# Softmax of a cross-attention in a four-part block: exponential taken on the transposed tile, sums by products with ones, division behind the values

## The reference

```python
def _L1_xattn_ref(q, k, v, mask, Wq, bq, Wk, bk, Wv, bv, Wo, bo):   # 16 heads of 16, 64 keys
    qh, kh, vh = (proj(q, Wq, bq), proj(k, Wk, bk), proj(v, Wv, bv))
    scores = jnp.einsum('bhqd,bhkd->bhqk', qh, kh) / jnp.sqrt(jnp.float32(D_K))
    scores = jnp.where(mask == 0, jnp.float32(-1000000000.0), scores)
    attn = jax.nn.softmax(scores, axis=-1)
    x = jnp.einsum('bhqk,bhkd->bhqd', attn, vh)
    x = x.transpose(0, 2, 1, 3).reshape(N, -1, NUM_HEADS * D_K)
    return x @ Wo.T + bo
x = x + _L1_xattn_ref(_layernorm(x, axis=-1), ctx_1024, ctx_1024, mask_1x1xSxS2_ik1, ...)
x = x + _L1_ffn_ref(_layernorm(x, axis=-1), ...)
```

## Time and profile before

| what | value |
|---|---|
| time, median of 3 runs | 870.63 us (866.11 to 880.41) |
| the profiled execution's own time | 869.87 us |
| its span, first to last instruction | 868.1 us |
| TensorE busy (share of the span) | 783.3 us (90%) |
| VectorE busy | 453.0 us (52%) |
| ScalarE busy | 254.9 us (29%) |
| GpSimd busy | 181.8 us (21%) |
| second attention and gate, about 563 to 676 us | 113 us |
| in it: PE, DVE, ACT, POOL busy | 90.64, 91.55, 58.39, 54.30 us |

### The profile page before, as it was taken

How to read it: one execution, slowest core, us unless ns; L and a number is a source line. 1 busy time by engine, 2 the same in 40 slices (tenths; PEclk the granted TensorE clock), 3 DMA queues, 4 the chain that set the end, 5 groups by cost and what they waited for, 6 DMA issues and landing times.

```text
span 868.1 us, 11371 instructions
## 1 busy us (share of the span) xinstructions
PE 783.3 (90%) x4207; PEld 636.9 (73%) x4207; DVE 453.0 (52%) x866; ACT 254.9 (29%) x500; POOL 181.8 (21%) x180
## 2 busy tenths in 40 slices
PE   5999797888898999999999999978787399999996
PEld 4665475667687878887888788845566399999995
DVE  3565759796772394349335833497966511111111
ACT  1534213022311222123112312256534043333331
POOL 3022224240200020002000200176531212222221
PEclk9989988989899999999999999999979599999999
DMA  9951600000400000000000000053013477666640
GB/s 313 384 185 69 271 1 2 0 1 17 178 2 1 2 2 3 2 2 2 2 2 2 2 2 3 2 237 151 27 46 113 160 261 219 209 211 216 213 160 0
DMA packets 20525, 79.69 MB, mean 92 GB/s; under 512 B 3053, under 2 KB 12400, under 8 KB 15664
## 3 DMA queue, kind: packets, MB, share of 16 engines
q1 hardware_dynamic: 17504, 70.44, 23.5%
q0 software_dynamic: 2944, 8.13, 2.4%
HBM read 72.27 MB, written 18.74 MB: 105 GB/s over the span
## 4 chain that ended last, share of the span: by engine, by line
PE 70%; DVE 21%; issue 4%; ACT 3%; DMA 1%; POOL 0%; DVEq 0%; SPq 0%; ACTq 0%; POOLq 0%
PE ps L1063 29%; PE ps L1769 10%; PE ps L1781 9%; PE ps L526 4%; PE ps L498 3%; DVE head_max L1611 2%; DVE any_bits L307 2%; DVE stats L282 2%; DVE f_ha_hi L1183 1%; DVE f_raw L1177 1%; DVE c_tok L1612 1%; PE ps L555 1%; PE ps L480 1%; PE ps L1221 1%; DVE a_tok L847 1%
## 5 line engine op out<-in xcount | busy, mean ns | idle before, releaser
L1151 ACT ACTIVATE f_raw<-ps,cols 128x512 f32<-128x512 f32 x96 | 66.2, 690 | 261.7 <-PE ps L1063 242.6
L1063 PE MATMUL ps<-f_hb_hi,fh 128*128 128x512 f32 x256 | 101.2, 395 | 2.5 <-DVE inexact L327 2.5
L1063 PE MATMUL ps<-f_ha_hi,fh 128*128 128x512 f32 x256 | 99.9, 390 | 2.3 <-ACT f_raw L1151 2.3
L1063 PE MATMUL ps<-f_hb_lo,fh 128*128 128x512 f32 x256 | 100.6, 393 | 0.0
L1063 PE MATMUL ps<-f_ha_lo,fh 128*128 128x512 f32 x256 | 99.6, 389 | 0.0
L1769 PEld LDWEIGHTS ps<-xsT,ew 128*128 128x128 f32 x736 | 87.0, 194 | 2.8 <-DVE xsT L1896 1.7
L1769 PE MATMUL ps<-xsT,ew 128*128 128x128 f32 x736 | 87.5, 278 | 1.0 <-DVE xsT L1896 1.0
L1829 ACT ACTIVATE hT<-ps,ew 128x128 f32<-128x128 f32 x184 | 52.5, 369 | 106.2 <-PE ps L1769 96.6
L1781 PE MATMUL ps<-ew,hT 128*128 x368 | 83.3, 380 | 0.0
L1183 DVE CAST f_ha_hi<-f_raw 128x512 fp32r<-128x512 f32 x64 | 31.9, 498 | 89.4 <-ACT f_raw L1151 88.3
L1781 PEld LDWEIGHTS ps<-ew,hT 128*128 128x128 f32 x368 | 68.2, 190 | 8.7 <-issue 0.2
(11 more groups left out here) (235 smaller groups left out, 1280.7 us busy)
## 6 DMA issues: line engine op xcount, KB each, us to landing
ew<-in_ew SPq DMA_DIRECT2D x23, 1028.0 KB, 5.7
fh<-fh_copy SPq DMA_DIRECT2D x2, 4096.0 KB, 14.8
ew<-in_ew SPq DMA_DIRECT2D x1, 8192.0 KB, 23.6
fw<-fw_copy SPq DMA_DIRECT2D x3, 1024.0 KB, 6.8
eb<-in_eb SPq DMA_DIRECT2D x23, 128.0 KB
x_res<-in_x SPq DMA_DIRECT2D x4, 512.0 KB, 10.6
rows<-x_res SPq DMA_DIRECT2D x4, 512.0 KB, 3.3
rows<-xn_e SPq DMA_DIRECT2D x4, 512.0 KB, 3.1
```

The costliest lines, as they stand in the source:

```text
L1063: ins = nc.tensor.matmul(out, *((xk, wk) if swap else (wk, xk)), start=(k == 0 and part == 0), stop=(k == w.shape[1] - 1 and part == 1))
L1151: nc.scalar.activation(f_raw[:, m % 3, :], ps[:, ring_bank(n), :], ACT.Silu if m < KH else ACT.Gelu, scale=col(("w1_s", "h1_s", "h2_s")[m ...
```

## The change

The softmax of the second attention is taken in another order.

- `c_tok` has one buffer; `subtract_max` is as before. `probabilities(b, j)` now transposes one tile's undivided logits, eight groups of 128 by 128, four into bank 0 and four into bank 1, and ACT takes the exponential while it copies them to `c_pT` (`exponentials`). ACT's in-place exponential, its plain copies and DVE's copies of the last batch are gone.
- `invert_sum` and `divide` are gone. `heads` runs, beside each of the value products, a second product of the same size with ones (`vmask`) as the weights; each head's sum comes out in banks 6 and 7, repeated over the head's 16 rows. `invert_sums` on DVE takes the reciprocals of those banks, 128 by 512 each, two a batch, to `c_sums`, and `scale_heads` on POOL multiplies `c_oT` by them.
- The last batch does this in two halves of 256 tokens (`last_heads`): DVE takes reciprocal and product straight from PSUM, POOL takes no part.
- All the orders are rewritten. Transposes of batch `b` now follow its own scores, heads and projection of batch `b - 1` lie in the iteration of batch `b`; a projection lags by one batch, not by two.

The core of the diff:

```diff
-        c_tok = [at(f"c_tok{i}", [P, TT, H1, KEYS], kb) for i, kb in enumerate((157.5, 101.5))]
+        c_tok = at("c_tok", [P, TT, H1, KEYS], 157.5)
+        c_sums = at("c_sums", [P, NG1, S], 113.5)
...
-            def divide(b, j):
-                pool.wait_ge(c_inv, TT * b + j + 1)
-                p = c_tok[b % 2][:, j]
-                pool.tensor_tensor(p, p, head_sum[:, j, :].unsqueeze(2).broadcast_to([P, H1, KEYS]), ALU.mult)\
-                    .then_inc(c_prob, 1)
+            def scale_heads(b):
+                for o in range(NG1):
+                    pool.wait_ge(c_pv_out, NG1 * b + o + 1)
+                    pool.wait_ge(c_inv, NG1 * b + o + 1)
+                    pool.tensor_tensor(c_oT[:, o, :], c_oT[:, o, :], c_sums[:, o, :], ALU.mult).then_inc(c_heads, 1)
...
+            def probabilities(b, j):
+                n = b * TT + j
+                pe.wait_ge(c_sub, n + 1)
+                if j == 0:
+                    if b < LAST:
+                        pe.wait_ge(c_q_out, NG1 * (b + 2))
+                    else:
+                        pe.wait_ge(c_pv_out, NG1 * b)
+                for h in range(2):
+                    if j:
+                        pe.wait_ge(c_pT_out, 2 * (n - 1) + h + 1)
+                    for m in range(TT):
+                        heads = c_tok[:, j, 8 * h + 2 * m:8 * h + 2 * m + 2, :].rearrange("p a k -> p (a k)")
+                        ins = nc.tensor.transpose(ps[:, h, m * P:(m + 1) * P], heads, ident)
                     ins.then_inc(c_pT_full, 1)
+
+            def heads_and_sums(b, o, columns, heads_out, sums_out):
+                for q in range(TT):
+                    m = q // 2 * TT + 2 * o + q % 2
+                    rows_ = slice(q * 2 * DH1, (q + 1) * 2 * DH1)
+                    nc.tensor.matmul(heads_out[rows_], v1_blocks[:, b % 2, o * TT + q, :], c_pT[:, m, columns],
+                                     start=True, stop=True)
+                for q in range(TT):
+                    m = q // 2 * TT + 2 * o + q % 2
+                    rows_ = slice(q * 2 * DH1, (q + 1) * 2 * DH1)
+                    ins = nc.tensor.matmul(sums_out[rows_], con("vmask", 2 * DH1), c_pT[:, m, columns],
+                                           start=True, stop=True)
+                return ins
...
+            def last_heads(hf):
+                if hf == 0:
+                    pe.wait_ge(c_values, NG1 * B)
+                    pe.wait_ge(c_sub, TT * LAST + 3)
+                pe.wait_ge(c_pT_out, 2 * TT * LAST + 4 * (hf + 1))
+                for o in range(NG1):
+                    bank = (2 if hf == 0 else 0) + o
+                    ins = heads_and_sums(LAST, o, slice(hf * D, (hf + 1) * D), ps[:, bank, 0:D], ps[:, bank, D:2 * D])
+                ins.then_inc(c_pv_full, 1)
...
+            for b in range(LAST):
                 scores(b, 0)
+                if b:
+                    heads(b - 1)
                 scores(b, 1)
-                if b < LAST:
-                    attn1_columns(pe, b + 1)
-                if b >= 2:
-                    project(b - 2, 0)
-                    project(b - 2, 1)
-                if b < LAST:
-                    attn1_queries(pe, b + 1)
+                attn1_columns(pe, b + 1)
+                attn1_queries(pe, b + 1)
                 scores(b, 2)
...
+                    project(b - 1, 0)
+                    project(b - 1, 1)
                 scores(b, 3)
...
+                probabilities(b, 0)
+                probabilities(b, 1)
+                if b:
+                    project(b - 1, 2)
+                probabilities(b, 2)
+                if b:
+                    project(b - 1, 3)
+                probabilities(b, 3)
+            scores(LAST, 0)
+            heads(LAST - 1)
+            scores(LAST, 1)
+            scores(LAST, 2)
+            probabilities(LAST, 0)
+            project(LAST - 1, 0)
+            probabilities(LAST, 1)
+            project(LAST - 1, 1)
+            scores(LAST, 3)
+            last_heads(0)
+            project(LAST - 1, 2)
+            probabilities(LAST, 2)
+            project(LAST - 1, 3)
+            probabilities(LAST, 3)
+            project(LAST, 0)
+            project(LAST, 1)
             gate_columns(0)
...
+            last_heads(1)
...
+            def exponentials(b, j):
+                for h in range(2):
+                    act.wait_ge(c_pT_full, 2 * (b * TT + j) + h + 1)
+                    if j == 0 and b:
+                        act.wait_ge(c_pv_full, NG1 * b)
+                    nc.scalar.activation(c_pT[:, h * TT:(h + 1) * TT, j * P:(j + 1) * P],
+                                         ps[:, h, :].rearrange("p (m n) -> p m n", m=TT), ACT.Exp).then_inc(c_pT_out, 1)
...
-            def invert_sum(b, j):
-                dve.wait_ge(c_exp, TT * b + j + 1)
-                if b:
-                    dve.wait_ge(c_prob, TT * (b - 1) + j + 1)
-                sums = head_sum[:, j, :]
-                s_order.step(nc.vector.tensor_reduce(sums, c_tok[b % 2][:, j], AX.X, ALU.add))
-                nc.vector.reciprocal(sums, sums).then_inc(c_inv, 1)
+            def invert_sums(b):
+                for o in range(NG1):
+                    dve.wait_ge(c_pv_full, NG1 * b + o + 1)
+                    if b:
+                        dve.wait_ge(c_heads, NG1 * (b - 1) + o + 1)
+                    nc.vector.reciprocal(c_sums[:, o, :], ps[:, 6 + o, :]).then_inc(c_inv, 1)
+
+            def last_heads(hf):
+                dve.wait_ge(c_pv_full, NG1 * LAST + hf + 1)
+                dve.wait_ge(c_heads, NG1 * LAST)
+                dve.wait_ge(c_wo_full, TT * (LAST - 1) + 2 * (hf + 1))
+                tokens = slice(hf * D, (hf + 1) * D)
+                for o in range(NG1):
+                    bank = (2 if hf == 0 else 0) + o
+                    s_order.step(nc.vector.reciprocal(c_sums[:, o, tokens], ps[:, bank, D:2 * D]))
+                    ins = nc.vector.tensor_tensor(c_oT[:, o, tokens], ps[:, bank, 0:D], c_sums[:, o, tokens], ALU.mult)
+                ins.then_inc(c_half, 1)
```

214 lines of the change are left out of this document (78 added, 136 removed).

## The result

| what | before | after |
|---|---|---|
| time, median (lowest to highest), 7 runs each on one chip | 866.94 us (866.11 to 880.41) | 875.33 us (873.58 to 878.98) |
| ratio of after to before, 95% interval | | 1.0095 [1.0068, 1.0121] |
| the profiled execution's own time, its span | 869.87, 868.1 us | 878.98, 877.2 us |
| PE, DVE, ACT, POOL busy, whole span | 783.3, 453.0, 254.9, 181.8 us | 797.2, 456.5, 240.4, 158.8 us |
| first logits to last gate logits | 109.78 us | 115.29 us |

The 880.41 us of before is one execution in a slower state, which the ratio leaves out. The change costs 8.4 us of 867, some 1%. The forecast was 872 with a range from 860 to 881, so the time lies within it, on the upper side. The sum behind it was less good than its total: its errors partly cancelled, and that was luck. What follows takes the sum apart.

A forecast was written before the change was run, and what follows sets the result against it. DVE was taken as the second attention's chain, PE close behind. A gain of 2.7 us against 4.5 lost to the clock gave +1.8 on 869.87, 871.7; with the median 0.8 above, 872, range 860 to 881.

The forecast's parts named there:

- The reciprocal: DVE's added reciprocals in the second attention: 3.35 us for 128x512, 1.75 for 128x256, 27.1 us together.
- The rivals of a fast and of a slower one: DVE's reciprocal at copy pace, total 859 us, chance 0.12; or 8.35 ns an element, total 880, chance 0.06.
- The first batch: Second attention's start: table load, then eight exponentials with transposes under them; DVE gets the second batch's first logits at 578.8.
- The middle batches: Two batches after the first: DVE is the chain at 21.75 us each, above PE's 21.1, ending at 622.3.
- a PE batch is 20.1 us: PE's work per batch in the second attention, summed from its groups; 21.1 with about 1.0 of waiting for ACT's copies.
- The last batch: DVE's work up to `last_heads(1)`: 33.1 us, with 0.3 of small waits, ending at 655.7 before clock losses.
- The two falls of the clock: Lower PE clock after waits before `project(2, 0)` and `project(3, 0)`, delaying DVE's maximum and `last_heads(1)` by 2 us each.
- The tail: The gate's remainder after the last batch, up to the last gate logits: 16.2 us, to 671.9 before clock losses.
- the third fall: Lower PE clock after a 3 us wait before `ranks_inside(0)`, costing `project(3, 2)` 0.5 us.
- The early fall: Rival: clock already low when `heads(0)` begins, later batches start 1.5 to 3.5 us later, total 875; chance 0.12.
- the slowest case: Rival: lower clock through the middle batches into the last, one PE batch 41 us, total 888 or more; chance 0.04.
- Nothing lost to the clock: Rival: clock falls absent or hidden under DVE's work in the second attention, total 867 to 869; chance 0.16.

The follow-up runs named there:

- e_warm: Changed kernel plus six unread filler products in each of PE's three waits of 3 us; 869.44 us, 1.0011 of the kernel before.
- e_best: Changed kernel with batch 0's ranks behind the last projections, the exponential's table loaded early and filler products in five places; 865.82 us, 0.9987 of the kernel before.
- e_ranks: Changed kernel with the ranks of batch 0 moved behind the last two projections on PE; 871.39 us, 1.0036 of the kernel before.
- before_again: The kernel before, unchanged, run and traced a second time; 866.08 us, ratio 0.9978.
- e_table: Changed kernel with the exponential's table loaded early, while ACT waits for the first batch's queries; 873.39 us, 1.0066 of the kernel before.
- before_warm: The kernel before with unread filler products in its own PE waits of the second attention; 866.49 us, ratio 0.9986.
- e_best_ln: e_best with ACT instead of DVE inverting the sums of the last two batches, as exp(-ln(s)); 876.12 us, 1.0087 of the kernel before.

## Why the forecast came out as it did

**The reciprocal** was the deciding term and it was right: 3.32 us for 128x512 and 1.75 for 128x256, where the line through two sizes of 12 and 16 elements gave 3.35 and 1.75. The rivals of a fast and of a slower one are excluded. An element costs (3.320 - 1.752) / 256 = 6.1 ns. The Trainium skill ("VectorE: DVE Perf Modes", "First, the fixed hardware budget") gives the reciprocal a repeat count of eight. My estimate from it, eight cycles an element or 8.3 ns and 4.4 us, does not agree with this case's rows.

**The first batch** was forecast at 13.9 and took 14.85. ACT's exponentials began where they should, 8.91 us after the first logits against 8.93. The step that failed is "eight exponentials of 0.54 follow, PE transposes under them": both wait for each other. A tile takes 1.41 us, from 576.73 to 578.14, not 1.08, since each hand-over adds 0.32 on one engine and 0.34 on the other. Three times the 0.33 are the 1.0 us.

**The middle batches** were forecast at DVE's 21.75 and took PE's 21.99. The step "a PE batch is 20.1 us" was short by 0.8, as PE was busy 20.92; the waits of 1.0 were right, and DVE's own 21.4 to 21.5 nearly so. Half of it is the price of the scores, taken from pairs: two tiles of scores in a row take 2.36, but one between other groups takes 1.28 (581.28 to 582.56 in PE's timeline), and in the new order each of the four stands so, 5.1 for the 4.72 forecast. Of the rest 0.2 is the pair of projections between two scores, 1.92 for 1.73 (616.14 to 618.06), 0.16 the columns and 0.1 the transposes, while the heads took 0.1 less. The error was of little effect, 0.5 us over two batches, only because two bounds were close; the same closeness makes the reciprocals cost nothing there. The sign that DVE is the chain, under 5 us of idle time from 579 to 656, did not come: in the same 77 us, 3 later in this trace, DVE was idle 8.6.

**The last batch** was forecast at 33.4 without the clock, and e_warm and e_best, which keep it up, have 33.26 and 33.27. The two falls of the clock came at the two waits named, with lengths of 2.99 and 3.09 us for the 3 expected. DVE waited 1.25 and 1.70 us behind them where I had 2 and 2, and the piece is 2.6 longer than in e_warm, for the 4 forecast.

**The tail** is the term that was mis-sized: 16.2 plus 0.5 for the third fall, and it took 20.56. I had let that fall last for one projection. It lasted to the end of the stage, over the projections, all the gate logits that were left and the gate's columns, and DVE waited 4.56 us for one slice of them. The length was carried over from one short stretch in the trace of before. Why the clock came back within 5 us behind the first two waits and not behind the third, no run shows. The last gate logits came at 683.11, and 115.3 us behind the first ones, where 672 to 678, or 107 to 113 us, was the sign of the forecast.

**The base** was the other miss, and its sign was the opposite. The sum was made against the first trace of before. That execution had lost 2.9 us to the lower clock in its last batch, which another one did not. The forecast of +1.8 us compares with +5.5 between the first traces, and with +8.4 between the medians and between the second traces. In steps: first batch +0.9, middle +0.5, last batch -1.5, tail +3.9 make 3.8 of stage (115.29 for the 111.5 forecast), and 2.9 are the base. The absolute figure of 872 was nearer than either, because the 870.63 from which it started was high for this kernel. That the time lies in the range is therefore in part luck: the range had been opened upwards for other reasons, an early fall of the clock and a slower line, and neither of them came.

**The early fall**, the rival with the slowest case behind it, did not come: the clock was 1.00 in every window from 560 to 622. "Nothing lost to the clock" is excluded by e_warm, which gains 5.3 us of stage.

## What to carry to other kernels

In this kernel a reciprocal cost DVE about 6 ns for every element of a partition, nearly five times a copy at 512 elements. So count the elements before a division is moved behind products with ones: here each sum was divided on 16 equal rows, and that took back all that was freed (an inversion of each sum once was not tried). Price a new order on both engines that take turns, with each hand-over and with the shorter groups that it makes, and look for waits of PE on the path, since the lower clock behind them cost this kernel 5.3 us. For a difference of 1%, compare the lengths of stages, and take two traces of the old kernel first.

## What the runs showed of the hardware

- The reciprocal of 128x512 out of PSUM took 3.294 to 3.357 us and of 128x256 1.746 to 1.758, within 1% of the line through the 12 and 16 element ones in SBUF. A copy of 128x512 in its place took 0.691.
- After each wait of PE of 2.96 to 3.09 us the granted clock fell to the lower level, at once or within 2 us. The length of the wait alone does not decide it: a lower pace also followed waits of 1.66 us (e_ranks), 1.92 and 2.65 (before), and full pace followed 2.58 (before_again) and 2.79. The same wait of 2.99 us was followed by a first group at full pace in after and at half pace in e_table, whose last batch was 1.2 us longer. Products that nobody reads kept the clock at 1.00 until 654, and it paid where PE's work behind the wait was on the path (5.3 us) and not in the kernel before (before_warm).
- Gate logits, 16 products of 8 columns each, take 3.4 to 3.6 us at the lower clock and 1.93 at the full one, so such short products are nearly as sensitive to it as long ones (3.75 against 1.89 for eight of 128x256).
- In e_best_ln ACT loaded a table each time it went from the exponential to the logarithm or back, 1.28 us each, six times in the last batch.
